# Gated recurrence on one core: TensorE's score products of a half group in one burst

## The reference

```
def step(Smat, inp):
    qt, kt, vt, gt = inp
    Smat = Smat * jnp.exp(gt)[..., None] + kt[..., None] * vt[..., None, :]
    o = jnp.einsum('...k,...kv->...v', qt, Smat)
    return (Smat, o)
```

## Time and profile before

| | us |
|---|---|
| median of 3 runs | 2689.44 |
| lowest, highest | 2684.31, 2692.98 |
| the profiled execution | 2683.82 |
| its span | 2682.1 |

### The profile page before, as it was taken

The page is one execution under the profiler, slowest core; times in us unless marked ns, Lnnn a source line. Parts: engine busy times, 40 slices in busy tenths (PEclk is TensorE's granted clock), DMA queues, the critical chain, the costliest instruction groups (busy, mean ns, idle before and its releaser), DMA issues. The chain is left out here.

```text
span 2682.1 us, 79472 instructions
## 1 busy us (share of the span) xinstructions
PE 2271.7 (85%) x30000; PEld 1484.3 (55%) x30000; DVE 1851.7 (69%) x4635; ACT 1556.0 (58%) x3824; POOL 1530.2 (57%) x3168
## 2 busy tenths in 40 slices
PE   8799999999999999998759934489999998786793
PEld 5445555555555555546538823366776766664583
DVE  6578888888888888874445564277777776573456
ACT  5577777777777777772323321366666665553231
POOL 3357777777777777778545546444554444255452
PEclk9889999999999999999789955699999998887897
DMA  6911111111121111103437562201111111642456
GB/s 216 265 31 39 39 38 38 39 38 39 38 66 39 38 39 39 38 21 119 158 107 230 177 217 107 96 22 51 51 51 51 51 39 35 222 155 75 147 151 228
DMA packets 188728, 243.87 MB, mean 91 GB/s; under 512 B 41672, under 2 KB 144981, under 8 KB 187456
## 3 DMA queue, kind: packets, MB, share of 16 engines
q1 hardware_dynamic: 161824, 182.08, 22.5%
q0 software_dynamic: 19872, 50.41, 5.4%
q10 hardware_dynamic: 6656, 6.31, 0.7%
HBM read 136.08 MB, written 106.50 MB: 90 GB/s over the span
## 5 line engine op out<-in xcount | busy, mean ns | idle before, releaser
L724 DVE TENSOR_REDUCE at_mn<-at_S 128x1 f32<-128x1024 f32 (+4 forms) x704 | 612.2, 880 | 156.7 <-PE at_S L823 152.2
L658 ACT ACTIVATE at_E<-at_S,at_mn 128x1024 f32<-128x1024 f32 (+4 forms) x704 | 596.4, 848 | 202.6 <-DVE at_mn L724 200.8
L865 PE MATMUL at_pcs<-at_E,at_c 128*32 128x256 f32 (+1 forms) x4864 | 435.0, 347 | 0.0
L823 PE MATMUL at_S<-am_sk,am_sq 96*128 96x512 bf16 (+3 forms) x1152 | 334.2, 354 | 28.1 <-ACT at_E L658 23.2
L597 POOL TENSOR_TENSOR at_kvo<-am_kh,am_vh 128x256 f32<-128x256 f32 x512 | 303.7, 627 | 0.0
L1332 POOL DMA_INDIRECT expert_out<-m_ysb,m_dst x158 | 155.4, 983 | 143.2 <-issue 76.2
L865 PEld LDWEIGHTS at_pcs<-at_E,at_c 128*32 128x32 f32 x4864 | 186.8, 109 | 87.2 <-issue 81.6
L582 POOL TENSOR_TENSOR at_half<-at_half 128x128 f32<-128x128 f32 (+4 forms) x640 | 185.3, 290 | 50.1
L865 PE MATMUL at_pcs<-at_Tt,at_c 128*32 128x128 f32 x1024 | 209.7, 287 | 0.0
L648 ACT ACTIVATE at_Tt<-at_S,at_mn 128x192 f32<-128x192 f32 x512 | 173.4, 426 | 45.9 <-DVE at_mn L714 45.8
L823 PEld LDWEIGHTS at_S<-am_sk,am_sq 96*128 96x128 bf16 x1152 | 78.5, 97 | 203.6 <-issue 116.0
(11 more groups left out here) (392 smaller groups left out, 5530.1 us busy)
## 6 DMA issues: line engine op xcount, KB each, us to landing
m_xg<-expert_rows SPq DMA_DIRECT2D x158, 129.0 KB
am_sq<-q_parts SPq DMA_DIRECT2D x192, 64.0 KB, 2.3
am_sk<-k_parts SPq DMA_DIRECT2D x192, 64.0 KB, 2.2
memory_rows<-m_blank SPq DMA_DIRECT2D x16, 516.0 KB
gl_hx<-memory_rows SPq DMA_DIRECT2D x32, 258.0 KB, 3.4
m_wgu<-in_f_wgu SPq DMA_DIRECT2D x2, 4096.0 KB
rt_yin<-expert_out SPq DMA_DIRECT2D x7, 1024.0 KB, 11.9
fn_yin<-expert_out SPq DMA_DIRECT2D x7, 1024.0 KB, 8.5
```

Source lines behind the costliest of these rows:

```text
L658: nc.scalar.activation(E[:, at:at + w], S[v % NS_B][:, 0:w], ACT.Exp, bias=mn[:, q, s, 1 + j:2 + j], scale=-1.0, accum_out=rs[:, q, s, 1 + ...
L724: nc.vector.tensor_reduce(mn[:, q, s, 1 + j:2 + j], S[v % NS_B][:, 0:w], AX.X, ALU.min).then_inc(s_mn, 1)
L823: ins = nc.tensor.matmul(S[v % NS_B][:, c:c + cw], sq[:, u, t * P:(t + 1) * P], sk[:, u, c0 + c:c0 + c + cw], start=True, stop=True)
L865: ins = nc.tensor.matmul(pcs[j * R:(j + 1) * R, cols[0]:cols[1]].rearrange("p (b c) -> p b c", c=P), lhsT, rhs, start=(n, j) not in touche ...
```

## The change

TensorE's hand-written order in `phase_gla` changes, on no other engine. The five score calls of each half group stand directly behind one another. In the first half, `query(i+1)` and `output(i-1, 1)` stood between them, and now stand behind them, the output first. In the second half, `value(i+1, 0)` stood between them and now stands ahead of `scores_base(i, 1)`, and `output(i, 0)` stands behind `scores_far(i, 1)`.

```
             for i in range(NG):
                 more = i + 1 < NG
                 scores_base(i, 0)
-                scores_half(i, 0, 4)
-                scores_half(i, 0, 8)
+                for blk in (4, 8, 16):
+                    scores_half(i, 0, blk)
+                scores_far(i, 0)
+                if i:
+                    output(i - 1, 1)
                 if more:
                     query(i + 1)
-                scores_half(i, 0, 16)
-                if i:
-                    output(i - 1, 1)
-                scores_far(i, 0)
-                if more:
                     key(i + 1, 0)
                 if i:
                     carry_out(i - 1, 1)
                 if more:
                     key(i + 1, 1)
                 key_T(i)
-                scores_base(i, 1)
                 if more:
                     value(i + 1, 0)
-                scores_half(i, 1, 4)
-                scores_half(i, 1, 8)
+                scores_base(i, 1)
+                for blk in (4, 8, 16):
+                    scores_half(i, 1, blk)
+                scores_far(i, 1)
                 output(i, 0)
-                scores_half(i, 1, 16)
-                scores_far(i, 1)
                 if i + 2 < NG:
                     rows_T(i + 2)
```

## The result

| | us |
|---|---|
| after, median of 4 runs | 2721.59 (2717.27 to 2733.35) |
| before, beside it | 2690.61 (2684.31 to 2692.98) |
| ratio | 1.0113, 95% interval 1.0093 to 1.0134 |
| the profiled execution after | 2721.14, before 2683.82 |

The account below looks back on a forecast made before the run. It took TensorE, the busiest engine, to bound the loop, with a ScalarE and VectorE ring close behind. Terms 31 - 10 - 6 - 8 - 3 = +4 us gave a median of 2693 us, range 2676 to 2709.

Parts of the forecast that it names:

- Instruction feed, +31: TensorE's 48 dense score stretches: each pays 1.0 us for late instruction packets, less 17 us paid now; +31 us.
- The expected look: Profile after: TensorE "issue" waits at 40 to 60 us, some before output rows; instruction packets stay near 109.
- Wait on `keep_far`, -10: Before scores_base(i, 1): the value product moved ahead covers ScalarE's copy, removing all 10.3 us of wait; -10 us.
- State update, -6: Before key_T: earlier scores let VectorE's mask and update come sooner, saving 6 of 7.9 us; bounds 0 and 7.9.
- Empty queue, -8: At the turn's head: short stops after the keep_far wait, 12 us, shrink by two thirds; -8 us, bounds 0 and 12.
- Fewer changes of kind, -3: TensorE's switches between product kinds: 0.14 us each, most replaced by others, one or two fewer per turn; -3 us.
- Rival A2: Faster: all eight changes of product kind per turn are saved, 26 us instead of 3; 2670 us, chance 0.05.
- The clock, no term: Gated recurrence loop: TensorE's clock is granted at 0.98, so it was given no cost.
- Rival B: Clearly slower: instruction feed costs its middle price per dense stretch, about +16 us; 2706 us, chance 0.31.
- a turn can't be shorter than 22.1 us: Loop turn: ScalarE's and VectorE's own work from gates to next gates sets a 22.1 us minimum.
- the cap of 19 us on any gain: Loop: the ScalarE and VectorE ring allows at most 0.8 us gain per turn, 19 us in all.
- rivals A: Faster: instruction feed does not bind, waits on keep_far and the state update go; about -16 us, 2673, chance 0.12.

Follow-up runs that it names:

- tail: Changed kernel plus 512 more score products (1024 matmul rows) behind the loop's last output; 2751.45 us, one run.
- shift: Changed kernel plus 64 identity transposes (128 instructions, half a packet) ahead of the loop; 2732.09 us, single run.
- half1: Kernel before with only the second half group changed: value product first, then all its scores, then the output; 2694.26 us, ratio 1.0009.
- carry: Changed kernel with carry_out(i-1, 1) moved ahead of key(i+1, 0); 2714.71 us, ratio 1.0094.
- grain: Kernel before plus coarse and fine stretches of the same score and wide products behind the loop; first coarse 56 us, first fine 48.7, second coarse 48.7.
- half0: Kernel before with only the first half group changed: its scores together, output and query behind them; 2726.84 us, ratio 1.0141.
- h0q: Kernel before with only output(i-1, 1) moved behind the first half's scores, query left where it was; 2694.66 us, ratio 1.0001.
- afterq: Changed kernel with the query put back behind 96 of the first half's 176 score rows; ratio 1.0040, on another chip.
- spaced: Against the kernel before, TensorE's order in both halves spaced out, with wide products between shorter runs of scores; 2692.04 us, ratio 1.0004.

## Why the prediction was wrong

Its sum was +31 - 10 - 6 - 8 - 3 = +4 us. The loop grew by 34.7. Term by term:

- **Instruction feed, +31.** Held, a little under-sized: 48 x 1.0 less 17 was the forecast, 41 stops of 1.24 us less the 15 of before is what came, +36. With the short stops at the turns' heads all "issue" waits grow by 34.4 us. tail and shift show the mechanism. The expected look came true too: 27.0 us of these waits now stand before output rows, where there were hardly any, and the packets are 102 in the 530 us, with less work in them.
- **Wait on `keep_far`, -10.** Held: 13.8 to 5.5 us over the loop, -8.3. half1 shows it by itself.
- **State update, -6.** Failed: 7.9 to 7.6. The step said that the mask comes earlier once the scores do. It does; but the carry product, which the change leaves behind scores, output, query and key, then comes last. The prediction looked only at VectorE's waits of before and not at what is late next; carry took 6.5 us of this wait away by moving that product.
- **Empty queue, -8.** Failed. The pairs of short stops mostly stay: two under 0.5 us within 1.3 us stand 11 times in the loop before (8.4 us) and 8 times after (6.5 us), so -2. The reason given was a wait on `keep_far` just ahead; the pair at 2005.77 (0.31 and 0.44) has no such wait ahead of it. What makes the pairs stays open.
- **Fewer changes of kind, -3.** Too small by a factor of six or seven. The price of 0.14 us was right (grain: 0.18), the count was not: "Most are replaced by another change" is wrong. By the table a turn has 11 before and 5 after: 6 x 23 x 0.16 = 22 us. Measured piece by piece (each piece of a turn at 2.4 GHz and without a stop, in both orders, added up over the loop) it is 19 us. Rival A2, at 26, was nearer, though its eight changes are six.
- **The clock, no term.** This is the step that failed most: "The clock is granted at 0.98 there, so it is no part of the story." That holds for before. Clock not given in the loop is 24 us before and 46 after, +22; the part of it in which TensorE stood idle anyway, some 2 us, costs nothing, so about +20. It falls on the output rows, whose busy time grows from 130.8 to 159.4 us. From 1800 to 2290 us the level falls 12 times after. Nine of these falls begin inside one of the 36 stops of 0.5 us and more of that stretch, or within 2 us behind it; the other 27 stops have none, and three falls come behind short stops near a turn's head. Before, from 1800 to 2260 us, the level falls 3 times, each time near short stops at a turn's head, and none of the 14 longer stops has one.

In sum: 34.4 - 8.3 - 0.3 of waits and 2.6 of small ones are the 28.4 us of idle time. Clock and changes of kind, 20 - 19, leave 1 us of the 6.3 of busy time; the other 5 are for the most part what a stop costs beyond its length (in grain a stop of 2.20 us makes its period 2.44 longer, one of 1.68 us 1.83).

Rival B foresaw the side, and its size would fit the loop without the clock: 34.7 - 20 is some 15 us, and B said 16. That is luck. B's feed was 41 to 50 us more than before, where 36 came; it took 8 us each for the update (the forecast took 6) and the empty queue, where 0 and 2 came, and 3 for the changes of kind, where 19 came. The 15 us are worked out, not run: no run here holds the clock. With the clock at +20 the forecast would have been +24, near the 31 measured; a part of that nearness would be luck too, since three other terms were off.

One bound of the prediction is not shown by its rows: that a turn can't be shorter than 22.1 us "whatever TensorE does". Between the two ends that the earlier trace rows shows ScalarE also waits for TensorE:

```profile
1993.94 0.59 ACT L2327 COPY gl_ysb<-gl_O 128x512 f32<-128x512 f32 x1 [0.96 <-PE gl_O L2645]
```

So the cap of 19 us on any gain, which rivals A and A2 use, is not proven. No run here came near it.

What stays open: why both halves together cost no more than the first alone (loops +34.7 against +35.6, while the second alone has +8.3). Part is in the table: half0 keeps three changes of kind more and waits 4 us longer on L2303. And I can't say which stop brings the clock down: that the stops do it at all rests on the nine falls that begin at one and on the kernels in which both grow together, and grain has a stop of 2.20 us without a fall.

## What to carry to other kernels

Where small products stand in long runs, count them against the rate of the instructions, here 128 matmul rows per 3.74 us, before you join them. A wide product between them gives the next packet time to arrive: with the query left among the scores (h0q, afterq) nearly all or most of the loss was gone. More of the same is not better: spaced has wide products in more places and is not faster than before. When an edit makes stretches with stops in them, price the clock for the products behind, whatever clock the profile of before shows. Count changes of kind along the whole turn in both orders, and when a wait is to go, follow the whole chain to what comes last in the new order.

## What the runs showed that I had not expected

- One packet of instructions per 3.74 us, a stop after every 128 matmul rows, and no "issue" wait before score products longer than 2.4 us in any kernel of the table: as if only the next packet is on its way while one is used up. 128 score rows take 1.47 us at 2.4 GHz in tail, and 3.74 less 1.47 is 2.3, the stop that follows them there. This reading is not the whole: shift has one stop of 4.38 us inside its scores (2128.39).
- That rate against the Trainium skill: "Advanced Engine Details and Errata", ISA Cache, gives TensorE 128 KB. The stop after each 128 rows in tail, 16 KB of loads and matmuls, speaks against a long store that is filled ahead.
- With 1.7 us of stop in every 3.74, TensorE was granted 0.50 for 29 us on end.
- Coarse and fine grain cost the same to 0.1 us where the clock held: 3.9 us of stops against 24 changes of kind.
